# A one-pass gate, a later set-up, and expert outputs added in pairs on VectorE

## The chip, the cores and the metric

The kernel runs on one core of one Trainium2 chip. The metric is device time in microseconds (us) for the whole program: three runs of the kernel before took 2207.76, 2207.96 and 2212.83 us, median 2207.96.

## The reference, cut to what matters

A batch of 16 images (64 channels, 128 x 128) goes through three stages, all in fp32. 1024 image tokens come from deformable attention, 128 text tokens are appended, so each image has 1152 tokens of 64 channels.

```
q_feat = bilinear_sample(image, grid);  q = q_feat @ W_q.T
off    = gelu(layer_norm(q_feat @ W_o1 + b_o1)) @ W_o2 + b_o2      # 8 points for each query
s      = bilinear_sample(image, grid + 4 * off);  k = s @ W_k.T;  v = s @ W_v.T
h      = concat(softmax(q . k) @ v, txt)                           # [16, 1152, 64]
h      = h + Re(C_w @ state) + d_vec * n(h)    # time axis is the batch: 16 steps, state per token
x      = n(h)                                  # n: normalisation over the 64 channels
logits = x @ gate_w + gate_b;  disp = the two largest, their probabilities scaled to sum 1, else 0
out    = h + sum over 16 experts e of disp[e] * ((silu(x @ w1[e]) * (x @ w2[e])) @ w3[e])
```

All 16 experts (hidden size 128) are computed for every token and weighted by `disp`.

## The kernel before, in words

The loop is over the 16 images. Tokens are handled in 9 tiles of 128, three tiles to a group (`GT = 3`, a group is 384 columns), so there are three groups to an image. Every engine runs an order of work that is written out by hand, one letter to a piece of work, in `ORDER` (lines 167 to 254); `KINDS` names the letters. Each engine is strictly in order, and semaphores join them. Stages of image b+1 (map, gather, attention) stand between the expert work of image b. No planner runs at build time.

The kinds of work that matter here, with their letters:

- `A1` (a): TensorE turns the map, four rows at a time, ScalarE stores it (`pixmaj`, line 913); `A2` (b) samples the grid. `B0` to `B6` compute offsets and the gather indices `idx`. On SyncE `L` (p) loads the map, `Q` (C) writes a quarter of the table of pixels to HBM. On GpSimd `G` (o) gathers points from the table (line 601), two indirect DMAs and a short memset (`rest`, line 608) at a time, 64 indirect DMAs to an image; `B1` (e) there computes one power.
- `D1` (k) on VectorE weights the four corners of gathered points (`wsam`, line 1138), `D2` (l) transposes them on TensorE and adds the corners, `D3` (m) makes keys and values, `S1` to `S3` and `D5` are the attention. `gath` has two buffers.
- `P1` to `P6` are the norms and the state update of a group. `P7` (z) is the gate: `xsplit` holds a token's x in 64 partitions rounded to fp32r and in the other 64 the rest; for each of the three tiles TensorE runs two matmuls with 16 columns into the same 16 columns of `bank_p`, one with the rounded gate weights, one with their rest (line 736); VectorE then adds the bias (line 1100) and finds the two largest. `P8` makes `disp`, `P9` transposes it.
- `X` (J), 16 to a group: four matmuls for h1 and h2 of one expert (lines 658, 659; three PSUM banks in turn), ScalarE's silu (842), VectorE's product into `hid` (1038), which has `HB = 4` slots.
- `R` (D), 8 to a group: TensorE spreads `disp` of two experts over 128 partitions, ScalarE stores it in `wide` (882).
- `W` (I), 8 to a group: TensorE makes the outputs of two experts in `bank_o`, one expert in each half of the partitions (667); VectorE multiplies by `wide` into `scaled[n % SB]` (1045), `SB = 5` buffers. The next `W` waits for that product, as `bank_o` is one bank.
- `Z` (K), 2 to a group: TensorE transposes four `scaled` buffers and adds them in `bank_z`, three tiles by four buffers, 12 matmuls (677). `M2` (q) on VectorE adds the two halves and the residual into `ob` (1057, 1058), and SyncE stores it.

At the start SyncE issues constants in four parts between the map's loads (`load_constants`). With them come `w1` and `w2` in raw form, 2 MB in four DMAs into the two `gath` buffers, and `w3` (0.5 MB). VectorE waits for all constants, splits `w1` and `w2` into rounded part and rest (`w12`, lines 960 and 961), and computes the phases of the state. TensorE's `setup()` stands before the first `A2` and waits for `setup_done`, which VectorE gives at line 987; ScalarE's `setup()` stands there as well. GpSimd's first gather waits for `setup_done` too, since the raw weights lie in `gath`.

Of the kernel before, what the change touches and what calls it, by code (L numbers as in the profile page):

```python
# [34 lines left out]
C = 64  # L35
# [10 lines left out]
NE = 16  # L46
# [11 lines left out]
HB = 4  # L58
PAIRS = NE // 2
HALF = PAIRS // 2  # L60
SB = 5
# [19 lines left out]
def grid():  # L81
# [87 lines left out]
        "aaaaaaaaaaaaaaaabbbbbbbbcdehiaaaaaaalalmmlaaalammllmamalaabbbbbbbblcmdmellmhmilaltmumvalaaalxamzJmaJ",  # L169
        "lJaBaDJIDJaDJlDImDJImDJalDJIDJKaJalamJmIlJJtIulvJmJImlxIzJKJaJBalDbJImDJImDJblDJIDJbDbJlDJmDImtJlubb",  # L170
        "bvJKIlbJmcJmdexlzIJlJImBJmDJlDIDJDDJKDIlDJmDJItmulJvhJiIJlJImamaJxaJKIJzaIJaJaJaaIBJDJDIDlDJKDJIDlDJ",
        "mDJItmuJlvJIJlJImJxmJKIlJzaJlIJmaBJmIDaJDlDIDJaDlJDamDJKDItmJuaJlIaJlvIJamJbmbJIbbbJbxbJKIblJzIlJcmJ",
        "BmJIDdDJlDJIDeDlDJmDJKDItmJuJlIJlvhJiImJamJaIJxaJKIJzaIJaaJJaaIBJDJDIDlDJKDJIDlDJIDmtJmuJlvJIJlIJmJx",
        "mJKIlJzaJlIJmaBJmIDaJDlJDIDalDJaDmJDKDItmJuaJlIaJlvIJamJbmbJIbbbJbxbJKIblJzIlJcmJBmJIDdDJlDJIDeDlDJm",
        "DJKDItmJuJlIJlvhJiImJamJaIJxaJaKIJzIaJaJaJaIBJDJDIlDJKDJIDlDJmDJIDmtJluJIvJlJImJKmxJIlJzaJlIJmaBJmID",
        "aJDlDIDJaDlJDamDJKDItmJuaJlIaJlvIJamJbmbJIbbbJbxbJKIblJzIlJcmJBmJIDdDJlDJIDeDlDJmDJKDItmJuJlIJlvhJiI",
        "mJamJaIJxaJKIJzaIJaaJJaaIBJDJDIlDJKDJIDlDJmDJIDmtJluJIvJlJImJKmxJIlJzaJlIJmaBJmIDaJDlDIDJaDlJDamDJKD",
        "ItmJuaJlIaJlvIJamJbmbJIbbJbbxbJKIblJzIlJcmJBmJIDdDJlDJIDeDlDJmDJKDItmJuJlIJlvhJiImJamJaIJxaJKIJzaIJa",
        "aJJaaIBJDJDIlDJKDJIDlDJmDJIDmtJluJIvJlJImJKmxJIlJzaJlIJmaBJmIDaJDlDJIDalDJaDmJDKDItmJuaJlIaJlvIJamJb",
        "mbJIbbbJbxbJKIblJzIlJcmJBmJIDdDJlDJIDeDlDJKDmDJItmJuJlIJlvhJiImJamJaIJxaJKIJzaIJaJaJaaIBJDJDIlDJKDJI",  # L180
        "DlDJIDmDJmtJluJIvJlJImJKmxJIlJzaJlIJmaBJmIDaJDlDJIDalDJaDmJDKDItmJuaJlIaJlvIJamJbmbJIbbJbbxbJKIblJzI",
        "lJcmJBmJIDdDJlDJIDeDlDJKDmDJItmJuJlIJlvhJiImJamJaIJxaJKIJzaIJaaJJaaIBJDJDIlDJKDJIDlDJmDJIDmtJluJIvJl",
# [120 lines left out]
def build(nc, x, txt, wq, wk, wv, w_o1, b_o1, ln_g, ln_b, w_o2, b_o2, nu, theta, bmat, cmat, dvec,  # L303
          gamma, gate_w, gate_b, w1, w2, w3, ident, stack, pick_in, refpx, interp, phase, out):
    with ExitStack() as ctx:
# [101 lines left out]

        const_in = sem("const_in")
        eye_in = sem("eye_in")
        raw_in = sem("raw_in")  # L410
        setup_v = sem("setup_v")
        setup_p = sem("setup_p")
        setup_a = sem("setup_a")
# [875 lines left out]
```

## Time and profile before

| | |
|---|---|
| runs, median (lowest to highest) | 2207.96 us (2207.76 to 2212.83) |
| the profiled execution, its own time | 2205.73 us |
| its span | 2203.9 us |
| TensorE matmul busy | 92% of the span |
| TensorE weight load busy | 70% |
| VectorE busy | 81% |
| ScalarE busy | 54% |
| GpSimd busy | 69% |
| mean granted TensorE clock | 0.977 of full speed |

The profile is one execution. Busy time of an engine is the union of its instructions, and what is left is waiting or the time between instructions. Weight loads overlap matmuls. `L677` is line 677 of the kernel before.

### The profile page before, as it was taken

To read this page: it belongs to the slowest core of one execution; us is meant where nothing else is said; L and a number is where in the kernel's file an instruction comes from. 1 tells how busy PE (TensorE), PEld (TensorE's weight loads), DVE (VectorE), ACT (ScalarE), POOL (GpSimd) and SP (SyncE) were. 2 spreads that over 40 slices of the span, in tenths; PEclk is the share of its full clock that TensorE was granted. 3 is DMA by queue.
4 is the path that set the end of the run, shared out by engine and by line. 5 is a ranking of instruction groups with operands and counts; after the bars stand their busy time and mean duration, and the time that the engine had idled before them with its cause. 6 is when DMAs were issued, how large, how long until landed. Compare 5 with 4: busy or idle time off the path is not lost.

```text
span 2203.9 us, 42639 instructions
## 1 busy us (share of the span) xinstructions
PE 2028.7 (92%) x13857; PEld 1541.3 (70%) x13857; DVE 1775.4 (81%) x4292; ACT 1184.9 (54%) x3048; POOL 1513.4 (69%) x1753
## 2 busy tenths in 40 slices
PE   2468999999999999999999999999999999999998
PEld 1346677777777777777777777777777677776765
DVE  1346788888889888888988888898988889898875
ACT  1225555555565555655555565555556556654553
POOL 0378778778686867868676786868688686868700
PEclk9778999999999999999999999999999999999999
DMA  8786726667654656656464666646476664632200
GB/s 196 218 240 171 214 74 186 178 179 197 168 156 116 188 161 186 195 165 174 121 192 133 188 197 172 184 121 194 119 201 176 179 191 126 184 95 75 71 3 6
DMA packets 363274, 346.61 MB, mean 157 GB/s; under 512 B 49456, under 2 KB 313776, under 8 KB 362928
## 3 DMA queue, kind: packets, MB, share of 16 engines
q1 hardware_dynamic: 313904, 209.60, 34.9%
q0 software_dynamic: 49152, 134.28, 21.0%
q8 instruction: 114, 1.87, 0.4%
q14 instruction: 104, 0.85, 0.1%
HBM read 205.90 MB, written 137.89 MB: 156 GB/s over the span
## 4 chain that ended last, share of the span: by engine, by line
PE 67%; DVE 12%; POOL 10%; issue 8%; ACT 2%; DMA 1%; POOLq 0%; DVEq 0%; ACTq 0%; SPq 0%
PE bank_h L658 11%; PE bank_o L667 10%; PE bank_h L659 9%; PE bank_d L748 9%; PE bank_d L758 9%; POOL gath L601 7%; PE bank_z L677 4%; PE bank_p L694 4%; PE bank_a L770 2%; DVE hid L1038 2%; DVE v_sb L1166 2%; DVE v_sb L1173 2%; PE bank_p L713 2%; PE bank_p L718 1%; POOL rest L608 1%
## 5 line engine op out<-in xcount | busy, mean ns | idle before, releaser
L601 POOL DMA_INDIRECT gath<-table,idx x1024 | 1133.9, 1107 | 258.5 <-issue 239.8
L658 PE MATMUL bank_h<-xsplit,w 128*128 128x384 f32 x1536 | 587.5, 382 | 18.7 <-DVE hid L1038 17.5
L659 PE MATMUL bank_h<-xsplit,w 128*128 128x384 f32 x1536 | 521.1, 339 | 0.0
L842 ACT ACTIVATE silu<-bank_h 128x384 f32<-128x384 f32 x768 | 382.5, 498 | 241.7 <-PE bank_h L659 239.7
L1038 DVE TENSOR_TENSOR hid<-silu,bank_h 128x384 f32<-128x384 f32 x768 | 419.9, 550 | 82.0 <-ACT silu L842 74.0
L658 PEld LDWEIGHTS bank_h<-xsplit,w 128*128 128x128 f32 x1536 | 293.0, 191 | 118.8 <-issue 63.8
L1138 DVE TENSOR_TENSOR wsam<-gath,cw 128x1024 f32<-128x1024 f32 x256 | 313.0, 1223 | 53.0 <-PE bank_d L748 27.0
L667 PE MATMUL bank_o<-hid,w_sb 128*64 128x384 f32 x1536 | 334.7, 514 | 12.2 <-DVE scaled L1045 10.8
L748 PE MATMUL bank_d<-eye,wsam 128*128 128x128 f32 x2048 | 275.7, 279 | 25.3 <-DVE wsam L1138 24.8
L659 PEld LDWEIGHTS bank_h<-xsplit,w 128*128 128x128 f32 x1536 | 293.7, 191 | 3.2
L758 PE MATMUL bank_d<-w_kv,samT 128*128 128x256 f32 x1024 | 278.5, 395 | 5.6 <-ACT v_sb L898 2.7
L748 PEld LDWEIGHTS bank_d<-eye,wsam 128*128 128x128 f32 x2048 | 237.5, 143 | 63.0 <-DVE wsam L1138 41.9
L882 ACT COPY wide<-bank_p 128x384 f32<-128x384 f32 x384 | 185.0, 482 | 161.8 <-PE bank_p L694 161.2
L770 PE MATMUL bank_a<-eye,xin 128*128 128x128 f32 x1024 | 171.4, 294 | 76.9 <-DMA xin<-x_dram 43.4
L621 POOL TENSOR_SCALAR lns<-lns 128x3 f32<-128x3 f32 x96 | 39.1, 408 | 293.4 <-ACT lnsq L848 289.4
L913 ACT COPY pixmaj<-bank_a 128x512 f32<-128x512 f32 x256 | 150.2, 587 | 139.9 <-PE bank_a L770 137.6
L1045 DVE TENSOR_TENSOR scaled<-bank_o,wide 128x384 f32<-128x384 f32 x384 | 212.2, 553 | 12.2 <-PE bank_o L667 8.1
L758 PEld LDWEIGHTS bank_d<-w_kv,samT 128*128 128x128 f32 x1024 | 181.3, 193 | 51.8 <-issue 22.1
L608 POOL MEMSET rest<- 1x400 f32 x512 | 215.9, 422 | 0.2
L770 PEld LDWEIGHTS bank_a<-eye,xin 128*128 128x128 f32 x1024 | 127.2, 149 | 114.7 <-issue 56.3
L1144 DVE TENSOR_TENSOR k_sb<-k_sb,q_sb 128x256 f32<-128x256 f32 x256 | 108.3, 423 | 114.8 <-ACT v_sb L898 114.0
L894 ACT COPY k_sb<-bank_d 128x256 f32<-128x256 f32 x256 | 95.3, 372 | 156.1 <-PE bank_d L758 155.0
(157 smaller groups left out, 2704.4 us busy)
## 6 DMA issues: line engine op xcount, KB each, us to landing
table<-pixmaj SPq DMA_DIRECT2D x80, 1024.0 KB, 9.7
xin<-x_dram SPq DMA_DIRECT2D x256, 256.0 KB
table<-pixmaj SPq DMA_DIRECT2D x32, 960.0 KB
table<-pixmaj SPq DMA_DIRECT2D x16, 1088.0 KB
gath<-table,idx POOLq DMA_INDIRECT x1024
out_dram<-ob SPq DMA_DIRECT2D x48, 96.0 KB, 7.0
gath<-w_dram SPq DMA_DIRECT2D x4, 512.0 KB, 9.5
interp_sb<-interp_dram SPq DMA_DIRECT2D x1, 1024.0 KB, 5.2
```

The source lines that it names most:

```text
L601: pool.indirect_dma_start(out=gath[buf][:, p, :, :].rearrange("p a c -> p (a c)"), out_offset=None, in_=table[par], in_offset=bass.Indirec ...
L608: nc.gpsimd.memset(rest[:], 0.0).then_inc(rested, 1)
L658: mm(bank[:, 0:GC], w12[:, e, which, 0, :], xsplit[gp][:], start=True, stop=False)
L659: mm(bank[:, 0:GC], w12[:, e, which, 1, :], xsplit[gp][:], start=False, stop=True).then_inc(ready, 1)
L667: last = mm(bank_o[C * h:C * (h + 1), 0:GC], w3_sb[:, 2 * q + h, :], hid[:, (2 * n + h) % HB, :], start=True, stop=True)
L748: last = mm(bank_d[:, 128 * (2 * f + pair):128 * (2 * f + pair + 1)], wsam[:, corner, 2 * pair:2 * pair + 2, :].rearrange("p n c -> p (n c)"),
L758: last = mm(bank_d[:, 256 * i:256 * (i + 1)], samT[:, 2 * f + i, :], w_kv[:], start=True, stop=True)
L770: last = mm(bank_a[:, 128 * r:128 * (r + 1)], xin[u % 2][:, HW * (4 * (c % 2) + r):HW * (4 * (c % 2) + r + 1)], eye[:], start=True, stop=T ...
L842: nc.scalar.activation(silu[e % 2][:], bank_h[r][:, 0:GC], ACT.Silu).then_inc(silu_done, 1)
L1038: tt(hid[:, n % HB, :], silu[e % 2][:], bank_h[r][:, 0:GC], ALU.mult).then_inc(hid_done, 1)
L1045: tt(scaled[n % SB][:], bank_o[:, 0:GC], wide[:, q, :], ALU.mult).then_inc(eo_scaled, 1)
L1138: tt(wsam[:].rearrange("p a n c -> p n a c"), gath[j % GB][:, 4 * f:4 * f + 4, :, :], spread(w, 3, C), ALU.mult).then_inc(weighted, 1)
```

## The change

Four edits.

1. **Pairs.** The product of an even `W` goes into one of two `paired` buffers, that of an odd `W` into `odd`; right behind an odd one VectorE adds `odd` into the even one's buffer. `Z` then transposes and adds two buffers instead of four, 6 matmuls instead of 12. `odd` is one buffer and `SB` is 2.
2. **Gate.** For each tile one matmul with 32 columns, the rounded gate weights and their rest side by side, instead of two with 16. VectorE adds the second half in an instruction of its own.
3. **Set-up.** The raw weights no longer go to `gath` but to `wide` and `hid`, and their DMAs, with that of `w3`, are issued after the fourth quarter of the first table. VectorE's phases, splits and rotation, ScalarE's and TensorE's parts of the set-up move into the `D1` and `D2` pieces of the first image. The first gather and the first `A2` no longer wait for the set-up, the first `X` waits for the splits.
4. **`HB = 6`** instead of 4, and new strings in `ORDER` for all five engines, with the same number of each letter. In an inner image the strings differ by a few neighbours changing places; at the start they differ more (GpSimd: 24 letters `o` between the first two `e` instead of 20).

```diff
-HB = 4
+HB = 6
-SB = 5
+SB = 2
-        scaled = [sb(f"scaled{i}", [128, GC]) for i in range(SB)]
+        paired = [sb(f"paired{i}", [128, GC]) for i in range(SB)]
+        odd = sb("odd", [128, GC])
...
# W on VectorE
-                        wait(dve, mix_ready, (n - SB) // HALF + 1)
-                        tt(scaled[n % SB][:], bank_o[:, 0:GC], wide[:, q, :], ALU.mult).then_inc(eo_scaled, 1)
+                        if q % 2:
+                            dve.wait_ge(eo_paired, n // 2)
+                        else:
+                            wait(dve, mix_ready, (n // 2 - SB) // 2 + 1)
+                        mine = odd if q % 2 else paired[n // 2 % SB]
+                        tt(mine[:], bank_o[:, 0:GC], wide[:, q, :], ALU.mult).then_inc(eo_scaled, 1)
+                        if q % 2:
+                            dve.wait_ge(eo_scaled, n + 1)
+                            even = paired[n // 2 % SB]
+                            tt(even[:], even[:], odd[:], ALU.add).then_inc(eo_paired, 1)
# Z on TensorE
-                        pe.wait_ge(eo_scaled, n + HALF)
+                        pe.wait_ge(eo_paired, (n + HALF) // 2)
...
-                            for q in range(HALF):
+                            for q in range(0, HALF, 2):
# P7 on TensorE and VectorE
-                            for part in range(2):
-                                last = mm(bank_p[:, NE * k:NE * (k + 1)], xsplit[gp][:, 128 * k:128 * (k + 1)],
-                                          gate_r[:, part, :], start=part == 0, stop=part == 1)
+                            last = mm(bank_p[:, 2 * NE * k:2 * NE * (k + 1)], xsplit[gp][:, 128 * k:128 * (k + 1)],
+                                      gate_r[:].rearrange("p a e -> p (a e)"), start=True, stop=True)
...
+                        link(top, tt(logit[:], parts[:, :, 1, :], logit[:], ALU.add))
# set-up: SyncE, TensorE, ScalarE, GpSimd, VectorE
-        raw_w = [gath[0][:].rearrange("p a b c -> p (a b c)"), gath[1][:].rearrange("p a b c -> p (a b c)")]
+        raw_w = [(0, 0, NE, flat[:, 0:NE * HID]), (1, 0, NE // 2, flat[:, NE * HID:NE * HID * 3 // 2]),
+                 (1, NE // 2, NE, hid[:].rearrange("p a b -> p (a b)")[:, 0:NE // 2 * HID])]
...
+                        if b == 0 and args[0] == 3:
+                            for dst, src in raw_loads:
+                                sp.dma_start(dst, src).then_inc(raw_in, 16)
...
+                        if n == 0:
+                            pe.wait_ge(split_v, 2 * len(raw_w))
...
+                        if b == 0 and (j, f) == (1, 1):
+                            setup()
...
-                if k == 0 and b == 0:
-                    pool.wait_ge(setup_done, 1)
...
+                            if (j, f) == (1, 0):
+                                setup_phases()
+                            elif (j, f) == (3, 0):
+                                setup_rot()
+                            elif (j, f) in ((1, 1), (2, 0), (2, 1)):
+                                split_weights(2 * j + f - 3)
```

## Rows read from the trace of the kernel before

**Rows 1.** The page, part 1: busy time and share of the span by engine.

```profile
PE 2028.7 (92%) x13857; PEld 1541.3 (70%) x13857; DVE 1775.4 (81%) x4292; ACT 1184.9 (54%) x3048; POOL 1513.4 (69%) x1753
```

**Rows 2.** By window: length, busy PE, PEld, DVE, ACT, POOL, then PEclk, DMA share, GB/s.

```profile
400.00:1800.00 1400.00, 1360.18 (x9531) 1046.39 (x9530) 1208.70 (x2927) 811.82 (x2092) 1043.77 (x1201) 1.00 0.60 168
```

**Rows 3.** Groups of TensorE, 400 to 1800 us: busy us, mean ns, idle before.

```profile
L677 PE MATMUL bank_z<-eye,scaled 128*128 128x128 f32 x792 | 97.4, 273 | 0.2
L736 PE MATMUL bank_p<-gate_r,xsplit 128*128 128x16 f32 x198 | 24.1, 242 | 0.0
```

**Rows 4.** VectorE's waits, 400 to 1800 us, first and last of 11: total, times, longest.

```profile
DVE k_sb L1144 <- ACT v_sb L898: 59.9, 63, 1.4
...
DVE dispr L1126 <- DVE disp L1123: 0.2, 1, 0.2
```

**Rows 5.** Groups of VectorE over the whole span, by shape.

```profile
L1045 DVE TENSOR_TENSOR scaled<-bank_o,wide 128x384 f32<-128x384 f32 x384 | 212.2, 553 | 12.2 <-PE bank_o L667 8.1 <-ACT wide L882 0.8
L1026 DVE TENSOR_TENSOR x2n<-lnx,lns 128x384 f32<-128x384 f32 x48 | 26.6, 555 | 13.9 <-POOL lns L624 13.7
L1100 DVE TENSOR_TENSOR logit<-bank_p,gateb 128x48 f32<-128x48 f32 x48 | 9.7, 202 | 2.2 <-PE bank_p L736 2.1
L1187 DVE TENSOR_TENSOR off_b<-off_a 128x128 f32<-128x128 f32 x16 | 4.7, 293 | 0.5
L961 DVE TENSOR_TENSOR w<-gath,w 128x2048 fp32r<-128x2048 f32 x2 | 4.6, 2293 | 0.1
```

**Rows 6.** Busy time by window over one image, columns as in rows 2.

```profile
1000.00:1021.20 21.20, 21.20 (x138) 17.22 (x138) 18.97 (x52) 11.88 (x35) 16.03 (x19) 1.00 0.33 88
1021.20:1042.40 21.20, 21.20 (x156) 16.57 (x155) 17.03 (x30) 15.42 (x37) 18.20 (x19) 1.00 0.90 249
1042.40:1063.60 21.20, 21.01 (x218) 16.21 (x216) 18.88 (x53) 10.28 (x29) 17.90 (x24) 1.00 0.66 194
1063.60:1084.80 21.20, 21.20 (x130) 16.46 (x130) 18.19 (x49) 11.54 (x32) 7.37 (x8) 1.00 0.08 20
1084.80:1106.00 21.20, 17.75 (x110) 12.95 (x110) 20.51 (x55) 13.50 (x31) 18.09 (x21) 1.00 0.81 227
1106.00:1127.20 21.20, 21.20 (x127) 15.48 (x127) 16.73 (x32) 11.01 (x32) 17.18 (x23) 1.00 0.79 232
```

**Rows 7.** Busy time by window at the start and the end, columns as in rows 2.

```profile
0.00:70.00 70.00, 17.56 (x64) 11.45 (x64) 12.45 (x26) 11.02 (x21) 1.00 (x9) 1.00 0.88 216
80.00:90.00 10.00, 2.49 (x9) 1.42 (x8) 5.32 (x20) 1.09 (x4) 1.65 (x1) 0.57 0.00 1
90.00:130.00 40.00, 22.98 (x100) 16.82 (x100) 10.38 (x17) 10.51 (x22) 33.37 (x40) 0.67 0.99 277
200.00:400.00 200.00, 187.47 (x1231) 141.26 (x1229) 165.96 (x387) 114.00 (x292) 157.64 (x184) 0.99 0.63 179
2094.00:2203.90 109.90, 99.37 (x525) 65.32 (x523) 76.31 (x203) 49.38 (x130) 5.26 (x10) 0.97 0.02 5
```

**Rows 8.** Instructions in order of time at the start: start us, us, idle before.

```profile
27.19 7.40 SPq L554 DMA_DIRECT2D gath<-w_dram  x4
...
71.59 0.42 PE L640 MATMUL bank_p<-eye,b_st 128*64 128x128 f32 x1 [4.10 <-DVE hid L987]
...
90.56 1.24 POOL L601 DMA_INDIRECT gath<-table,idx  x1 [6.56 <-DVE idx L1218]
...
155.68 1.68 POOL L616 TENSOR_TENSOR off_s<-off_s,neghalf 128x8 f32<-128x8 f32 x1 [6.03 <-DVE off_s L1189]
```

**Rows 9.** A gather beside a VectorE instruction with two operands in SBUF.

```profile
161.22 2.23 DVE L1166 TENSOR_TENSOR v_sb<-v_sb,score 128x2048 f32<-128x2048 f32 x1
...
161.68 2.58 POOL L601 DMA_INDIRECT gath<-table,idx  x1 [0.30 <-issue]
```

**Rows 10.** Groups of GpSimd, 400 to 1800 us.

```profile
L601 POOL DMA_INDIRECT gath<-table,idx x705 | 783.5, 1111 | 173.2 <-issue 165.3 <-DVE idx L1218 7.5 <-DVE wsam L1138 0.3
L621 POOL TENSOR_SCALAR lns<-lns 128x3 f32<-128x3 f32 x66 | 27.3, 413 | 174.1 <-ACT lnsq L848 171.1
```

More of the change, by code:

```diff
@@ L540, in out_group @@
                              ob[gp][:]).then_inc(out_done[gp], 16)
-            raw_loads = [(raw_w[n][C * half:C * (half + 1), :].rearrange("c (e h) -> c e h", e=NE),
-                          w.rearrange("e c h -> c e h")) for n, w in enumerate((w1, w2)) for half in range(2)]
+            raw_loads = [(raw[C * half:C * (half + 1), :].rearrange("c (e h) -> c e h", h=HID),
+                          (w1, w2)[which][first:last].rearrange("e c h -> c e h"))
+                         for which, first, last, raw in raw_w for half in range(2)]
+            raw_loads.append((w3_sb[:], w3.rearrange("e h o -> h e o")))
             loads = [(dst, src, const_in) for dst, src in const_loads]
-            loads += [(dst, src, raw_in) for dst, src in raw_loads]
             loads += [(dst, src, const_in) for dst, src in block_loads]
@@ L955, in _ @@
             step(nc.vector.memset(state[:], 0.0))
-            dve.wait_ge(raw_in, 64)
-            for n in range(2):
-                raw = raw_w[n].rearrange("p (e h) -> p e h", e=NE)
-                step(vcopy(w12[:, :, n, 0, :], raw))
-                step(tt(w12[:, :, n, 1, :], raw, w12[:, :, n, 0, :].bitcast(F32), ALU.subtract))
             step(vcopy(sel[:].rearrange("p (e c) -> p e c", c=C), spread(lnsq[:, 0, 0:NE], 2, C)))
@@ new lines, in setup_rot, with split_weights @@
+            def setup_rot():
+                dve.wait_ge(setup_a, 6)
+                step(ts(col[:, 14:16], col[:, 14:16], col[:, 7:8], None, ALU.mult))
+                step(ts(rot[:, 0:C], eye2[:], col[:, 14:15], None, ALU.mult))
+                step(ts(rot[:, C:128], eye2[:], col[:, 15:16], None, ALU.mult))
+                dve.wait_ge(setup_done, 1)
+                assert su.n == SETUP_V
+            def split_weights(n):
+                which, first, last, raw = raw_w[n]
+                raw = raw.rearrange("p (e h) -> p e h", h=HID)
+                high = w12[:, first:last, which, 0, :]
+                if n == 0:
+                    dve.wait_ge(raw_in, 16 * (2 * len(raw_w) + 1))
+                vcopy(high, raw).then_inc(split_v, 1)
+                dve.wait_ge(split_v, 2 * n + 1)
+                tt(w12[:, first:last, which, 1, :], raw, high.bitcast(F32), ALU.subtract).then_inc(split_v, 1)
@@ L1112, in run @@
                         g = args[0]
-                        top.start(b, TOP_N * g + 4)
+                        top.start(b, TOP_N * g + 5)
                         dve.wait_ge(gap_tanh, NGRP * b + g + 1)
```

242 lines of the change are left out of this document (123 added, 119 removed).

## The prediction

> **What bounds the kernel now.** I read the page's busy times first. TensorE's matmuls fill 92% of the span and VectorE 81% [rows 1]. Between 400 and 1800 us TensorE is busy 1360.18 of 1400 us, VectorE 1208.70 [rows 2]. The 792 transposes of line 677 there are 11 images of 72 [rows 3], so an image takes 1400/11 = 127.3 us. Of that TensorE works 1360.18/11 = 123.7 and stands 3.6; VectorE works 109.9 and stands 17.4. The list of waits says how the 17.4 divide: its eleven pairs sum to 148.5 us, 13.5 to an image, the longest for ScalarE's `v_sb` [rows 4]; the other 42.8, or 3.9 to an image, are short pauses between dependent instructions that no engine can take away. So VectorE's floor is 113.8, TensorE's 123.7, and TensorE sets the pace. The windows of one image show that it isn't so everywhere. In five of six TensorE is full; in the fifth it is busy 17.75 of 21.20 and VectorE 20.51, the softmax [rows 6].
>
> The start is another regime. Until 90 us the first map, the constants and the first table go through the DMA engines (share 0.88, 216 GB/s to 70 us), TensorE is busy a quarter of the time, and between 80 and 90 us the DMA engines do nothing at all [rows 7] while offsets are computed; the first gather starts at 90.56 [rows 8]. Then gathers pace the work until TensorE fills; it is busy 187.47 of the 200 us from 200 on [rows 7], so this is at about 210. After 2094 there is only expert work, TensorE busy 99.37 of 109.90 [rows 7].
>
> **Pairs, on TensorE.** 792 matmuls of line 677 are busy 97.4 us [rows 3], 0.123 each. 36 of 72 to an image go: 36 x 0.123 = 4.4 us. **Gate.** 198 matmuls are busy 24.1 us, 0.122 each, whether that is 16 columns or the weight load of 128x128 [rows 3]. 9 of 18 to an image go, 1.1 us; the wider ones cost between nothing and twice their price (then the gain is nil); I take nothing, since 128 columns in line 677 cost the same 0.123. TensorE's work falls to 123.7 - 5.5 = 118.2.
>
> **What VectorE gets.** Twelve additions to an image, 128x384, both operands in SBUF. The same shape from SBUF took 555 ns, with one operand in PSUM 553 [rows 5]; bounds from further off are 293 ns for 128 columns and 2293 for 2048. I take 0.555, less 0.01 of overlap, plus the pause behind the odd product it waits for, 0.5 us over 16 [rows 5] or 0.03: 0.58 x 12 = 6.9 us. The gate's second addition is 0.20, with its pause 0.24, three to an image [rows 5]: 0.7. I sum them with slightly longer pauses to 7.9 (7.6 by the rows alone, 0.3 for the new wait of an even product on `Z`). The floor of VectorE becomes 113.8 + 7.9 = 121.7. So the two engines change places: 118.2 against 121.7.
>
> **The sum over the windows.** A mean floor is only reached if work can move freely. I add to each window of rows 6 a sixth of VectorE's additions and pauses, (7.9 + 3.9)/6 = 1.97, take 5.5/6 = 0.92 from TensorE, and keep the larger:
>
> - 20.9, 20.3, 20.9, 20.3, 22.5, 20.3. VectorE sets the first, third and fifth, TensorE the rest.
>
> They sum to 125.2, against 127.3: 2.1 us less to an image. The softmax window gets longer by 1.3, the others shorter. The order strings could spread VectorE's load (down to 121.7), and waits that neither floor holds could add (3.6 as now); I let these cancel. From 210 to 2094 us there are 1884/127.3 = 14.8 images: 14.8 x 2.1 = 31 us.
>
> **New waits.** With two pair buffers the third pair of a group waits for the whole first `Z`, which waits for the addition. Behind the waiting product on VectorE stand `hid` products, for which TensorE's `W` and, through the three banks, its `X` wait. Before, the fifth product needed no `Z`, the sixth did. The price is 0 where `Z` has run in time, and up to one `Z` (0.74) six times, 4.4 us, where not; I take the 0.3 above, as line 677 hardly idled (0.2 us in 792) [rows 3]. `HB = 6` I cost at nothing: `hid` waits for silu and not for a slot in any long wait; it may give back some of TensorE's wait on `W`. What ScalarE does is unchanged and its load is 54% [rows 1].
>
> **The start.** 2.5 MB of raw weights leave the stretch to 70 us: at its 216 GB/s [rows 7] that is 11.7 us. Their four big issues also hold SyncE's queue for 7.40 us [rows 8] in front of the fifth load of the map; that lies within the 11.7. The first `A2` no longer waits behind the set-up: TensorE stood 4.10 us for line 987 [rows 8], most of it saved, 3.7. The seven raw DMAs now go out behind the last quarter of the table, into the 10 idle us of the DMA engines; behind them on SyncE stand loads of the second map, which TensorE does not need before the gathers run. VectorE's splits go between the first `D1`s: two of 2048 columns at most 2.29 each, four of 1024 at most half that, below 9.2 us, and the phases and rotation 17 short ones of some 0.2, or 3.7. VectorE is busy 10.38 of 40 us there [rows 7], so they are hidden; if a third came into the gathers' path, it would be 4 us. GpSimd stood 6.03 us at 155.68 for an operand of its power [rows 8]; four more `o` (eight gathers) stand in front of that now, so part of this wait goes, between 0 and 6.0, I take 3. In 90 to 130 us the DMA engines are at 0.99 [rows 7], so not all of the earlier start survives; I take 1.4 off. Start: 11.7 + 3.7 + 3 - 1.4 = 17 us, bounds 4 and 22.
>
> **The end.** Over 109.9 us VectorE has room (76.31) [rows 7]; TensorE's 5.5 to an image is 5.5 x 109.9/127.3 = 4.8 us. At the very last `Z` an addition of 0.58 comes in and 0.74 goes.
>
> **The time.** 17 + 31 + 5 = 53 us. The profiled execution took 2205.7 us with its span of 2203.9; 2205.7 - 53 = 2152.7. The median of the runs lies 2.3 above it, so 2155.
>
> **Rivals.**
>
> - *All of TensorE's saving arrives.* The strings were rewritten for all engines, and VectorE's longest waits are for TensorE's results, which now come sooner [rows 4]. Then VectorE's floor of 121.7 plus a few tenths is the pace: 5.2 x 14.8 = 77, with start and end 99 us: 2109. Against it speaks window five.
> - *Only the start and the end gain.* The stages that VectorE bounds lose what the others gain: 22 us, 2186.
> - *VectorE's waits stay: slower.* Place: the middle of each image; in order behind each `W`, VectorE's added 7.9 pushes `hid`, TensorE's `X` waits, and VectorE still stands for `v_sb` and silu. If all 13.5 of waits stay, an image takes 121.7 + 13.5 = 135.2. It decides from 127.3 + 22/14.8 = 128.8, so from 7.1 of the 13.5 still left. With 9 left: 130.7, 3.4 x 14.8 = 50 - 22, so 2236. For it speaks that these waits are many and short (63 times, at most 1.4 us) [rows 4]; against it that an engine that runs late waits less. Weight loads are busy 1046.39 of 1400 us, 75%, VectorE 86% [rows 2]. The Trainium skill ("Perfetto Trace Analysis", Identifying the Most-Contended Engine) holds matmul busy time a bad measure, since matmuls are pipelined, and wants weight-load share instead; by it VectorE is the bound already, the 5.5 are worth nothing and the 7.9 are paid. By the windows [rows 6], where TensorE has no gap in four of six, I don't follow it.
> - *Gathers slow down.* A gather that began beside a VectorE instruction of 2.23 us with both operands in SBUF took 2.58 us instead of a mean of 1.111 [rows 9, 10]. The additions are 12 more such instructions, 12 x 0.55 = 6.6 us to an image on GpSimd. It is busy 1043.77/11 = 94.9 and spends 15.0 between gathers: 109.9 + 6.6 = 116.5, still under 125.2. Only if its 15.6 us of waits for the norms [rows 10] stay too is it 132.1, 4.8 x 14.8 = 71 - 22 slower: 2257. The Trainium skill ("SBUF — State Buffer", SBUF: two separate sides) says that a VectorE instruction with two SBUF inputs holds a port pair that GpSimd shares, and shuts it out for its whole length; on this rows 9 agree.
>
> **Chances.** Forecast 0.60; all of it 0.13; start and end only 0.12; VectorE's waits 0.11; gathers 0.04. The forecast's own range is 2130 to 2180. For 8 in 10 I take 2110 to 2195, which leaves out the two slower cases and a little of the first rival. A difference of 0.3%, 6.6 us, is about what a measurement can tell: faster 0.84, within it 0.04, slower 0.12.
>
> **What would show it.** Between 400 and 1800 us line 677 has 36 matmuls to an image and TensorE's share falls to 94 to 95%, VectorE's rises from 86% to about 94%; VectorE's waits for `v_sb` and silu shrink to about half. The additions last 0.55 us. TensorE now has waits on `hid` and on the pair addition. The first gather starts near 75 us. I am wrong if VectorE's share stays below 90% while the time hardly falls (its waits stayed), if the mean gather goes above 1.25 us, or if the first gather is not before 80 us.

## The result, and the profile after

The changed kernel took 2187.72 us (median of 4 runs, 2184.80 to 2189.38) against 2207.86 (4 runs, 2206.97 to 2212.83) for the kernel before on the same chip: ratio 0.9899, 95% interval 0.9880 to 0.9918. It is 20 us faster, where 53 us were forecast. The time lies inside the range given for 8 in 10 (2110 to 2195) and outside the forecast's own (2130 to 2180). Runs more than 1.5% above the fastest of the same kernel are left out of every ratio. The profiled span is 2187.6 us, 16.3 less than before.

To see where the 16.3 us fell I take VectorE's instruction that writes an image's gather indices (`idx`), once per image. First the row of the kernel before, then of the changed one, from the fourth image to the last; "a to b" are the first and last start in us.

```profile
L1218 DVE SCALAR_TENSOR_TENSOR idx<-xyf x13: 224/225/227, 447.4 to 1973.8; 128x64 int32<-128x64 f32 x13
```

```profile
L1262 DVE SCALAR_TENSOR_TENSOR idx<-xyf x13: 224/225/227, 428.5 to 1953.5; 128x64 int32<-128x64 f32 x13
```

Up to the fourth image the changed kernel is 18.9 us ahead. The twelve images between take 1525.0 instead of 1526.4 us: 127.08 each instead of 127.20. From the last `idx` to the end of the span it takes 234.1 instead of 230.1. So: start -18.9, middle -1.4, end +4.0. The forecast had -17, -31 and -5 (its middle began at 210 us). The middle is what failed.

The page's busy times and the window of the middle (400 to 1800 us), as in [rows 1] and [rows 2]:

```profile
PE 1978.7 (90%) x13137; PEld 1472.8 (67%) x13137; DVE 1866.7 (85%) x4534; ACT 1183.3 (54%) x3048; POOL 1518.2 (69%) x1753
```

```profile
400.00:1800.00 1400.00, 1331.77 (x9038) 1002.80 (x9037) 1270.86 (x3094) 809.62 (x2093) 1045.44 (x1201) 0.98 0.60 168
```

TensorE's busy time fell by 28.4 us over these 11 images, VectorE's rose by 62.2, and TensorE now stands idle for 68.2 us where it stood for 39.8. The granted clock is 0.98 where it was 1.00.

Part 4 of the page follows the work that ended last back through whatever released it. The shares of that chain, in the kernel before and then in the changed one:

```profile
PE 67%; DVE 12%; POOL 10%; issue 8%; ACT 2%; DMA 1%; POOLq 0%; DVEq 0%; ACTq 0%; SPq 0%
```

```profile
PE 41%; DVE 26%; POOL 20%; issue 11%; ACT 1%; DMA 1%; DVEq 0%; POOLq 0%; ACTq 0%
```

TensorE carried two thirds of the chain and now carries two fifths; VectorE and GpSimd have about doubled. No engine sets the pace of the changed kernel alone.

The groups that the change touches (busy us, mean ns, idle before; 400 to 1800 us), as in [rows 3, 5, 10]:

```profile
L688 PE MATMUL bank_z<-eye,paired 128*128 128x128 f32 x396 | 56.3, 279 | 0.1
L746 PE MATMUL bank_p<-gate_r,xsplit 128*128 128x32 f32 x99 | 13.2, 234 | 0.0
L1081 DVE TENSOR_TENSOR paired<-paired,odd 128x384 f32<-128x384 f32 x132 | 73.9, 560 | 4.5
L1077 DVE TENSOR_TENSOR paired<-bank_o,wide 128x384 f32<-128x384 f32 x132 | 72.9, 552 | 1.9 <-PE bank_z L688 0.5 <-PE bank_o L678 0.3
L608 POOL DMA_INDIRECT gath<-table,idx x706 | 796.8, 1129 | 174.0 <-issue 165.4 <-DVE idx L1262 8.4 <-DVE wsam L1182 0.2
```

The reader sees 36 transposes to an image instead of 72, 9 gate matmuls instead of 18, 12 additions of 0.56 us, and gathers that hardly got longer (1129 against 1111 ns). The waits of TensorE and then of VectorE in the same stretch (total us, times, longest):

```profile
PE bank_o L678 <- DVE odd L1077: 21.2, 12, 1.9
PE bank_h L667 <- DVE hid L1066: 13.9, 23, 0.8
PE bank_a L782 <- ACT pixmaj L932: 8.4, 11, 0.8
```

```profile
DVE k_sb L1188 <- ACT v_sb L917: 29.9, 43, 1.4
DVE hid L1066 <- ACT silu L857: 25.8, 47, 1.0
DVE x2n L1054 <- POOL lns L631: 17.0, 15, 3.3
```

`v_sb` fell from 59.9 [rows 4] to 29.9, as forecast; TensorE's longest wait is now for a scaled product: 21.2 us, where the kernel before had 8.1 us in 11 waits. The windows of one image, as in [rows 6], show where it lies:

```profile
972.00:993.20 21.20, 21.20 (x123) 15.56 (x122) 17.08 (x32) 10.62 (x32) 17.19 (x21) 1.00 0.34 102
993.20:1014.40 21.20, 20.78 (x127) 16.07 (x126) 18.75 (x55) 14.57 (x40) 17.76 (x23) 1.00 0.68 185
1014.40:1035.60 21.20, 21.13 (x237) 15.27 (x236) 19.82 (x36) 12.19 (x28) 18.18 (x21) 1.00 0.96 278
1035.60:1056.80 21.20, 21.20 (x136) 17.03 (x135) 20.37 (x62) 13.26 (x38) 14.51 (x15) 1.00 0.20 57
1056.80:1078.00 21.20, 20.43 (x119) 14.55 (x117) 20.38 (x52) 13.27 (x32) 9.67 (x13) 1.00 0.26 68
1078.00:1099.20 21.20, 16.85 (x92) 13.05 (x93) 19.87 (x53) 10.23 (x27) 17.20 (x20) 0.92 1.04 294
```

In the last window, the softmax stretch, TensorE is busy 16.85 us (17.75 before), and there the clock is 0.92. TensorE's instructions in order of time (start, us, idle before) show the pause and what follows:

```profile
1082.25 0.33 PE L667 MATMUL bank_h<-xsplit,w 128*128 128x384 f32 x1
1082.42 0.34 PE L668 MATMUL bank_h<-xsplit,w 128*128 128x384 f32 x1
1082.60 0.60 PE L782 MATMUL bank_a<-eye,xin 128*128 128x128 f32 x4
1085.13 0.87 PE L678 MATMUL bank_o<-hid,w_sb 128*64 128x384 f32 x4 [1.94 <-DVE odd L1077]
...
1088.37 0.53 PE L668 MATMUL bank_h<-xsplit,w 128*128 128x384 f32 x1
1088.68 0.53 PE L667 MATMUL bank_h<-xsplit,w 128*128 128x384 f32 x1
...
1090.83 0.34 PE L705 MATMUL bank_p<-dispT,sel 128*128 128x384 f32 x1
```

A matmul of 384 columns takes 0.34 us before the pause and 0.53 behind it, and the next one starts 0.31 us later instead of 0.17: the granted clock is 1.2 instead of 2.4 GHz there. Adding up the stretches in which half speed was granted, between 400 and 1800 us: 13.7 us in the kernel before (4 stretches), 58.0 us in the changed one (13 in 11 images). My estimate is that half of such a stretch is lost: 6.8 against 29.0 us of full-speed work, 0.6 against 2.6 to an image.

VectorE's instructions in the same pause say what it stands for. The first row is the sum over the eight samples (three additions), the third the product that TensorE's `bank_o` waits for:

```profile
1081.66 2.40 DVE L1217 TENSOR_TENSOR v_sb<-v_sb 128x1024 f32<-128x1024 f32 x3
1084.10 0.43 DVE L1221 TENSOR_TENSOR h_sb<-v_sb,sden 128x256 f32<-128x256 f32 x1
1084.44 0.55 DVE L1077 TENSOR_TENSOR odd<-bank_o,wide 128x384 f32<-128x384 f32 x1
```

VectorE did these three in this order in the kernel before too. There TensorE had two pieces of the map (`a`) in front of that `W`, and waited little:

```profile
1098.90 0.60 PE L770 MATMUL bank_a<-eye,xin 128*128 128x128 f32 x4
1100.27 0.63 PE L770 MATMUL bank_a<-eye,xin 128*128 128x128 f32 x4 [0.77 <-ACT pixmaj L913]
1101.44 0.87 PE L667 MATMUL bank_o<-hid,w_sb 128*64 128x384 f32 x4 [0.54 <-DVE scaled L1045]
```

TensorE's old string has `aaI` at this place in 11 of 13 images. The new one has `JaI` in all 13, with one `a` moved elsewhere. So the pause of 1.9 us in front of this `W` comes with the new strings; the experiments bear this out.

### The profile page after: what moved, and what is told of

Read it like the earlier page. It is cut to its first block, busy times and chain, and to the rows that moved or that the text cites. A ratio compares the mean times of both kernels' runs of the same rounds, so it can differ in the third digit from the quotient of the medians.

```text
span 2187.6 us, 41444 instructions
## 1 busy us (share of the span) xinstructions
PE 1978.7 (90%) x13137; PEld 1472.8 (67%) x13137; DVE 1866.7 (85%) x4534; ACT 1183.3 (54%) x3048; POOL 1518.2 (69%) x1753
## 4 chain that ended last, share of the span: by engine, by line
PE 41%; DVE 26%; POOL 20%; issue 11%; ACT 1%; DMA 1%; DVEq 0%; POOLq 0%; ACTq 0%
POOL gath L608 15%; PE bank_h L667 7%; PE bank_o L678 6%; PE bank_h L668 6%; PE bank_d L760 6%; PE bank_d L770 5%; DVE hid L1066 4%; POOL rest L615 3%; DVE wsam L1182 3%; PE bank_p L705 3%; DVE v_sb L1217 2%; DVE v_sb L1210 2%; PE bank_z L688 1%; PE bank_a L782 1%; POOL lns L631 1%
## 5 line engine op out<-in xcount | busy, mean ns | idle before, releaser
L608 POOL DMA_INDIRECT gath<-table,idx x1024 | 1153.1, 1126 | 256.3 <-issue 239.5
L667 PE MATMUL bank_h<-xsplit,w 128*128 128x384 f32 x1536 | 594.0, 387 | 30.1 <-DVE hid L1066 26.9
L668 PE MATMUL bank_h<-xsplit,w 128*128 128x384 f32 x1536 | 526.6, 343 | 0.0
L667 PEld LDWEIGHTS bank_h<-xsplit,w 128*128 128x128 f32 x1536 | 297.7, 194 | 139.1 <-issue 69.9
L678 PE MATMUL bank_o<-hid,w_sb 128*64 128x384 f32 x1536 | 339.9, 520 | 34.8 <-DVE odd L1077 26.6
L668 PEld LDWEIGHTS bank_h<-xsplit,w 128*128 128x128 f32 x1536 | 298.5, 194 | 2.5
L628 POOL TENSOR_SCALAR lns<-lns 128x3 f32<-128x3 f32 x96 | 34.3, 357 | 274.5 <-ACT lnsq L863 270.1
L705 PE MATMUL bank_p<-dispT,sel 128*128 128x384 f32 x384 | 163.9, 427 | 2.5 <-ACT wide L897 2.3
L678 PEld LDWEIGHTS bank_o<-hid,w_sb 128*64 128x64 f32 x1536 | 78.7, 137 | 117.1 <-issue 98.7
```

The lines of the kernel that those rows point to most:

```text
L608: pool.indirect_dma_start(out=gath[buf][:, p, :, :].rearrange("p a c -> p (a c)"), out_offset=None, in_=table[par], in_offset=bass.Indirec ...
L667: mm(bank[:, 0:GC], w12[:, e, which, 0, :], xsplit[gp][:], start=True, stop=False)
L668: mm(bank[:, 0:GC], w12[:, e, which, 1, :], xsplit[gp][:], start=False, stop=True).then_inc(ready, 1)
L678: last = mm(bank_o[C * h:C * (h + 1), 0:GC], w3_sb[:, 2 * q + h, :], hid[:, (2 * n + h) % HB, :], start=True, stop=True)
L705: mm(bank_p[:, 0:GC], sel[:, 128 * q:128 * (q + 1)], dispT[:], start=True, stop=True).then_inc(wide_ready, 1)
```

## The experiments

Kernels were measured in five series, each on one chip with the kernel before beside them (the recorded expectations say "call"). In the last three series the kernel before took about 2210 us, and the traces of the edited kernels look like the two above. In the first two, with eight kernels on two chips, it took about 2380 us, and their traces have waits that nothing in the kernel ends (releaser `remote`). So every time is read against the kernel before of its own series. Two of these waits in the changed kernel, 400 to 1800 us:

```profile
ACT silu L857 <- remote: 36.8, 17, 7.2
ACT k_sb L913 <- remote: 13.0, 9, 2.2
```

### Two series with the kernel before at 2380 us

The edits, each on the changed kernel:

```
# no_add, no_add_again: an addition becomes a memset of 8 columns (the odd products are missing from the output)
-    tt(even[:], even[:], odd[:], ALU.add).then_inc(eo_paired, 1)
+    nc.vector.memset(odd[:, 0:8], 0.0).then_inc(eo_paired, 1)
# old_order, old_order_again: the ORDER strings of the kernel before
# u_pairs: pairs undone (scaled[n % 5], 12 transposes to a Z, HB = 4); order, gate, set-up new
# setup_gate: u_pairs with the old ORDER strings
# setup_only: setup_gate with the two-pass gate
```

> The changed kernel with the twelve additions to an image left out (the odd product is computed and not added, so the output lacks half of the expert outputs; 8 columns are cleared instead, to keep the signal). Theory A, VectorE is the bound between 400 and 1800 us now: it loses 12 x 0.56 = 6.7 us to an image less 12 short clears of some 0.07, so an image falls from 127.1 to 121 to 124 us and the time to 2115 to 2150. Theory B, the pace is set by GpSimd's order (gathers behind the waits for the norms) or another chain that the additions are not on: 2175 or more.

> The later set-up and the one-pass gate alone, with the order strings of before, four-buffer Z, SB = 5, HB = 4. Theory A (the pairs cost VectorE what they give TensorE): the start's 16 us and up to 1.1 us of TensorE to each of 15 images, so 2175 to 2190, no slower than the whole change. Theory B (pairs give something, the gain is lost in a fixed chain): 2192 to 2197, slower than the whole change.

> The later set-up alone, with the order strings of before. Both theories: the first index list comes some 15 us earlier, and 2208 - 12 to 16 = 2192 to 2196. If the strings of before give part of the start away again at GpSimd's wait (6 us), 2198 to 2202.

> The changed kernel with the order strings of before. Theory A: Z stands too early in TensorE's old order for the pair addition, TensorE waits more: 2195 to 2230. Theory B: the strings matter little in the middle, 2185 to 2195.

Measured in one series (before 2384.13): `no_add` 2285.13, ratio 0.9578 (0.9546 to 0.9610); `setup_gate` 2367.48, 0.9919 (0.9880 to 0.9959); `setup_only` 2369.82, 0.9933 (0.9902 to 0.9965); `old_order` 2330.72, 0.9792 (0.9750 to 0.9833). The changed kernel was not beside them, so its part in the 0.958 can't be told from these runs.

> The changed kernel itself, beside the others on one chip: the reference for this call. If TensorE runs here as in the first trace, 0.990 of the kernel before. If TensorE is held up more than there, as in the four runs of the call before (TensorE busy 89% of a span of 2366 us, with pauses of 1 to 2 us before single instructions), what lightens TensorE is worth more: 0.975 to 0.985.

> The changed kernel with the order strings of before, now beside the changed kernel. Theory A (Z stands too early for the addition): 1 to 2% slower than the changed kernel. Theory B (the strings matter little, the pairs do): within 0.5% of it.

> The changed kernel with the pairs undone: four scaled buffers to a Z, SB = 5, HB = 4, the new strings, the one-pass gate and the later set-up kept. Theory A (VectorE bounds the middle now, and the pairs take what they give): the same time as the changed kernel within 0.5%, TensorE's share back at 96 to 97%. Theory B (the pairs are a gain, the strings lose it): 1 to 2% slower than the changed kernel.

> The changed kernel with the twelve additions to an image left out, so that the output lacks half of the expert outputs, now beside the changed kernel. Theory A: an image falls from 127.1 to 121 to 124 us, 2 to 4% under the changed kernel. Theory B (a chain the additions are not on): within 0.7% of it.

Measured (before 2379.49): `after_again` 2259.95 and 2261.66, 0.9496 (0.9415 to 0.9577), its other two runs 2296.59 and 2303.89; `old_order_again` 2326.31, 0.9780 (0.9717 to 0.9842); `u_pairs` 2363.44, 0.9928 (0.9869 to 0.9986); `no_add_again` 2287.88, 0.9604 (0.9541 to 0.9667). There the change is worth 5% by its two lower runs. Undoing the pairs gives 103 of these 119 us back, and leaving out the additions gains nothing: it lies 27 us above the two lower runs, within the spread of all four. That is another regime, and nothing on the runs at 2210 us follows from it; all runs below have the kernel before at 2209 to 2213.

### Dummy work against the clock, and VectorE relieved

```
# fill: dummy transposes before six pieces of every order stretch "zIJaaJaJaI" (in 13 images), 3 5 3 5 12 4, 32 in all
+    if at.get(step, 0):          # at: the table of places; turned: the last D3 piece done (neither shown)
+        wait(pe, kv_stored, turned)
+    for _ in range(at.get(step, 0)):
+        mm(bank_d[:, 384:512], eye[:], eye[:], start=True, stop=True, is_transpose=True)
# no_vsum: the sum over samples on 2 of 32 columns
-    link(soft, tt(vw[:, :, 0:n, :], vw[:, :, 0:n, :], vw[:, :, n:2 * n, :], ALU.add))
+    link(soft, tt(vw[:, :, 0:n, 0:2], vw[:, :, 0:n, 0:2], vw[:, :, n:2 * n, 0:2], ALU.add))
# hb5_sb3
-HB = 6, SB = 2
+HB = 5, SB = 3
```

> The changed kernel itself, to compare the others of this call with. On the chip of its first profile it took 0.990 of the kernel before, on another chip 0.950, where TensorE is held up more. Here between 0.945 and 0.992.

> The changed kernel, with 32 dummy transposes of 128x128 per image (about 0.12 us each, 3.9 us in all) issued at six places of the softmax stretch where TensorE otherwise stands for VectorE and ScalarE, 6 us to an image. Theory C: what eats the forecast gain of the middle is the granted clock, which falls to half once per image just behind these pauses and costs 29.0 us of full-speed work between 400 and 1800 us instead of 6.8 before. Then the dummy work keeps the clock up and the time falls by 1 to 2 us per image, 15 to 25 us in all, or 0.7 to 1.1% against the changed kernel in this call, with less than half as much time at half clock. Theory V: VectorE's own chain sets the pace of the whole middle and the half clock hides beneath it. Then nothing comes back, and where a dummy outlasts the pause the kernel loses up to 1 us per image (0 to 15 us slower), even if the clock stays up.

> Leaves out nearly all of the sum over eight samples behind the softmax: three additions of 128x1024, 512, 256 columns (2.40 us together) shrink to 2 of 32 columns of each block, twice per image. VectorE's longest stretch without product or hid loses some 2 us each time. If VectorE in the softmax stretch is the pace and its pause costs the clock as well (theory C), the time falls by more than the 4 us per image that are left out: 4 to 5 per image, 60 to 75 us, 2.7 to 3.3% against the changed kernel. If VectorE's total work sets the pace (theory V), 4 per image, 55 to 60 us. If TensorE's count of instructions alone sets it and the pause does not matter, under 10 us.

> Three pair buffers instead of two and five silu-product buffers instead of six. If the new wait of an even product on Z (two buffers) is what holds the middle, it goes and the time falls by up to 0.5 us per image, 7 us (0.3%). By theories C and V alike nothing changes beyond 0.3%: TensorE waited 4.5 us in 12 times for a product into a pair buffer, 0.4 per image, of which only a part is for the buffer.

Measured (before 2212.69): changed kernel 2185.22, 0.9884 (0.9863 to 0.9906); `fill` 2174.01, 0.9834 (0.9813 to 0.9856); `no_vsum` 2164.12, 0.9777 (0.9752 to 0.9802); `hb5_sb3` 2185.17, 0.9893 (0.9862 to 0.9924).

`fill` adds work and is 11.2 us faster than the changed kernel. The `idx` rows of the changed kernel, `fill` and `no_vsum`, measured side by side; a twelfth of each stretch is an image, 126.76, 125.81 and 125.54 us:

```profile
L1262 DVE SCALAR_TENSOR_TENSOR idx<-xyf x13: 224/225/228, 425.8 to 1946.9; 128x64 int32<-128x64 f32 x13
```

```profile
L1280 DVE SCALAR_TENSOR_TENSOR idx<-xyf x13: 224/225/228, 425.5 to 1935.2; 128x64 int32<-128x64 f32 x13
```

```profile
L1262 DVE SCALAR_TENSOR_TENSOR idx<-xyf x13: 224/226/227, 425.6 to 1932.1; 128x64 int32<-128x64 f32 x13
```

The window of the middle of `fill` and TensorE's waits:

```profile
400.00:1800.00 1400.00, 1366.30 (x9480) 1035.11 (x9478) 1278.62 (x3128) 818.38 (x2118) 1053.29 (x1211) 1.00 0.60 169
```

```profile
PE bank_o L696 <- DVE odd L1095: 6.9, 11, 0.6
PE bank_h L685 <- DVE hid L1084: 5.4, 30, 0.3
```

The clock is back at 1.00 (3.4 us at half speed instead of 64.9 in the changed kernel beside it), and an image takes 125.81 instead of 126.76 us. The gain is below the 15 to 25 us of theory C. The dummies cost 50.4 us of TensorE in the middle (0.143 each, not 0.12); that some of it lay outside the pauses would explain the difference, but was not measured. Theory V, that the half clock hides beneath VectorE, is refuted, unless the dummies help by shifting TensorE's later work in time; no run adds such a shift and leaves the clock down.

`no_vsum` shrinks 4.7 us of additions per image to short ones of 1.1, so VectorE loses 3.6 us. 4 to 5 were expected back; 1.2 came (125.54), though the clock stayed up (6.8 us at half speed). `fill` got 1.0 with the clock up; if the clock is worth as much here, hardly anything is left for VectorE's 3.6 us. The pause in front of `W` is gone (one wait of 0.5 us for `odd`), so the sum over samples is what it stood for. Most of the 3.6 us turned into another wait of VectorE, which in the changed kernel beside it was 15.2:

```profile
DVE x2n L1054 <- POOL lns L631: 49.9, 22, 3.9
```

All three theories had the size wrong: even in the softmax stretch neither engine alone sets the pace. `hb5_sb3` is no faster (126.61 us to an image): a third pair buffer, with five `hid` slots instead of six, changes nothing.

### Additions, pairs and order, with the kernel before at 2209 us

The edits are those above; `fill_no_add` is `fill` with the additions left out as in `no_add`.

> The dummy transposes of the run before, and the twelve additions of an image left out (a memset of 8 columns on VectorE stands for each, so the output lacks the odd products). If VectorE's added work is what still holds an image at 125.8 us once the clock stays up (theory V), its 6.7 us to an image bring a good part of themselves: 2 us or more per image, 30 us and more, 0.969 of the kernel before or less. If what is left are waits that run through several engines (theory L: the norms from GpSimd, the softmax stretch, the order), it gives under 1 us per image, 0.976 to 0.983.

> The changed kernel with the pairs undone: eight scaled products in five buffers, 72 transposes of line 677 to an image, no additions, four silu-product buffers; the new order, gate and set-up stay. Theory C: TensorE's 4.4 us to an image come back, VectorE's 6.7 go, and TensorE no longer pauses so long in the softmax stretch, so the clock stays up: an image takes 127 to 128.5 us and the time is within 1% of the changed kernel's, 0.985 to 0.998 of the kernel before, with under half of the half-clock time. Theory T (TensorE's work alone counts, as on the chips where it is held up): 4.4 x 14.8 = 65 us slower than the changed kernel, 1.018 of the kernel before.

> The changed kernel without its twelve additions to an image (the output lacks the odd products). Theory C and L: the softmax stretch is VectorE's own softmax work, so TensorE's pause there stays and the clock still falls: under 1.5 us per image, 0.978 to 0.99 of the kernel before, and more than 25 us at half clock between 400 and 1800 us. Theory V: the additions are the pace, 3 to 5 us per image, 0.965 or less, and the clock stays up.

> The changed kernel with the order strings of the kernel before. Theory O: the rewritten strings carry part of the gain, as on the other chips (2%), through shorter waits: 1.00 to 1.01 of the kernel before, with TensorE waiting more than 10 us per image. Theory C: the strings matter less here; the start keeps most of its 16 us, an image takes 127 to 128 us, 0.99 to 1.0.

Measured (before 2209.39): `fill_no_add` 2151.83, 0.9733 (0.9717 to 0.9749); `u_pairs_once_more` 2196.05, 0.9939 (0.9922 to 0.9955); `no_add_once_more` 2164.93, 0.9792 (0.9776 to 0.9808); `old_order_once_more` 2216.47, 1.0028 (1.0012 to 1.0043). The `idx` rows of the last image stretch, in this order:

```profile
L1279 DVE SCALAR_TENSOR_TENSOR idx<-xyf x13: 224/225/227, 429.5 to 1922.9; 128x64 int32<-128x64 f32 x13
```

```profile
L1252 DVE SCALAR_TENSOR_TENSOR idx<-xyf x13: 224/224/226, 427.7 to 1958.7; 128x64 int32<-128x64 f32 x13
```

```profile
L1261 DVE SCALAR_TENSOR_TENSOR idx<-xyf x13: 224/225/226, 431.2 to 1934.1; 128x64 int32<-128x64 f32 x13
```

```profile
L1262 DVE SCALAR_TENSOR_TENSOR idx<-xyf x13: 224/226/228, 444.6 to 1978.4; 128x64 int32<-128x64 f32 x13
```

An image takes 124.45, 127.58, 125.24 and 127.82 us. Without the additions an image is 1.5 us shorter than the changed kernel's 126.76 (of the series before). They cost VectorE 6.7 (73.9/11 in the group above), and the memsets in their place 0.8, so 5.9 us are gone. So theory V, 3 to 5 us per image, is out; theory C's "under 1.5" is just met or just missed. With the clock kept up, `fill_no_add` is 1.4 us per image shorter than `fill`: between theory L (under 1) and theory V (2 or more), so both had it wrong. Without additions, TensorE's pause and the clock stay as they were: `bank_o` <- `odd` is still 21.2 us, and 58.0 us at half speed. The clock and the additions are nearly independent: the additions are worth 20.3 us without dummies (2185.2 to 2164.9) and 22.2 with them (2174.0 to 2151.8; the times of each pair are of two series, with before at 2212.7 and 2209.4). Undoing the pairs costs 11 us, as theory C had it. But its half-clock time, 44.4 us, is not under half of the changed kernel's, so the clock falls there too, without any addition. TensorE's wait in front of `W` in `setup_gate_once_more` (old strings, eight products), `u_pairs_once_more` (new strings, eight products) and `old_order_once_more` (old strings, pairs) shows with what the pause comes:

```profile
PE bank_o L676 <- DVE scaled L1071: 7.4, 9, 1.9
```

```profile
PE bank_o L676 <- DVE scaled L1071: 19.2, 11, 1.9
```

```profile
PE bank_o L678 <- DVE odd L1077: 7.7, 9, 1.9
```

It is 7 to 8 us with the old strings and 19 to 21 with the new ones, with pairs or without, with additions or without: the pause belongs to the order of work. Half speed was granted for 30.7, 44.4 and 41.0 us in these three, so this pause is a large part of the clock's loss but not all of it.

The old strings lose all of the gain: with them TensorE's waits are spread differently, the longest being

```profile
PE bank_p L695 <- DVE dispr L1164: 19.8, 20, 1.2
PE bank_h L667 <- DVE hid L1066: 17.7, 23, 1.2
```

and the fourth image is only 2.8 us ahead of the kernel before, though the first `idx` is at 76.7 instead of 90.0. Theory O was right on the time, though TensorE stands idle 7.0 us per image where it had said more than 10; theory C on the order was wrong.

### The end, and the set-up without the rest

```
# fill_tail: fill, and 73 dummies more at eight places of the order behind 1930 us
+    at.update({2622: 3, 2624: 16, 2625: 3, 2626: 11, 2627: 4, 2774: 26, 2817: 5, 2819: 5})
```

> The dummy transposes as before, and 73 more at eight places behind 1930 us: the last image's softmax stretch and three later pauses (4.04, 2.33 and 1.69 us are the longest). Theory C: at the end the clock costs 17 us of full-speed work instead of 9.3, and this is why the end did not gain its 5 us. Where the dummies keep it up, the end after the last idx falls from 235 us by 3 to 8, the time is 0.980 to 0.982 of the kernel before. If the end is held by VectorE's hid products and the pair additions in a row, the clock stays up and the time stays that of the run with dummies in the middle only, 0.983, or a little over.

> The order strings and the eight scaled products of the kernel before, with the new set-up and the one-pass gate only. On a chip where TensorE is held up it gave 0.992. With the old strings on top of all changes the third image was only 3 us early, though its first gather was 13 us early: so here, too, the set-up without new strings should bring under 6 us of its 13. Theory C: the gate's 1.1 us per image of TensorE mostly arrive, since VectorE has room (17.4 us per image idle): 10 to 16 us. Together 0.990 to 0.995. If the pairs under the old strings cost nothing of their own, it equals the run with the old strings, 1.003.

Measured (before 2209.79): `fill_tail` 2174.64, 0.9848 (0.9821 to 0.9875); `setup_gate_once_more` 2207.20, 0.9989 (0.9977 to 1.0001). The end of `fill` and then of `fill_tail`:

```profile
1935.00:2170.00 235.00, 211.33 (x1073) 141.74 (x1071) 194.84 (x483) 112.07 (x292) 98.60 (x117) 0.93 0.14 40
```

```profile
1935.00:2170.00 235.00, 218.90 (x1174) 150.91 (x1172) 198.49 (x494) 114.88 (x302) 98.74 (x118) 0.97 0.14 39
```

The half-speed time behind 1935 us fell from 37.3 to 17.1 us, which is some 10 us of full-speed work, but from the last `idx` to the end there are 233.6 instead of 235.5 us, and the time is the same. The 73 dummies are themselves 11.0 us of TensorE there, so this does not show that the clock costs the end nothing; it shows that dummies do not pay there. Leaving out the additions shortens the end to 229.8 us (`no_add_once_more`; 234.0 in the changed kernel of the series before).

`setup_gate_once_more` was expected at 0.990 to 0.995 and is no faster than before. Its `idx` row:

```profile
L1252 DVE SCALAR_TENSOR_TENSOR idx<-xyf x13: 224/225/227, 440.5 to 1971.6; 128x64 int32<-128x64 f32 x13
```

Its fourth image is 6.9 us ahead, and an image takes 127.59 us instead of 127.20, so the gate's 1.1 us of TensorE brought nothing. Part of that is the clock again: 30.7 us at half speed instead of 13.7, up to 0.8 us per image. The four corners, in us (kernel before 2209 to 2213):

| | time | fourth `idx` at | an image | last `idx` to the end |
|---|---|---|---|---|
| old strings, eight products, no additions | 2207.20 | 440.5 | 127.59 | 230.8 |
| old strings, pairs | 2216.47 | 444.6 | 127.82 | 235.8 |
| new strings, eight products, no additions | 2196.05 | 427.7 | 127.58 | 233.9 |
| new strings, pairs | 2185.22 | 425.8 | 126.76 | 234.0 |

All four have the new set-up and gate; `HB` is 4 with eight products and 6 with pairs, and no run separates that. Pairs alone cost 9 us, the strings alone bring 11, both together 22. The strings bring 13 us at the start, nothing in the middle while there are eight products, and cost 3 at the end. The pairs bring 0.8 us per image, 10 us in all, and only under the new strings. Each row is one trace; two traces of the changed kernel differ by 2.7 us at the fourth `idx` and by 0.3 us per image.

## Why the prediction was wrong, point by point

- **TensorE's work: nearly right.** Less what was lost to the clock, an image fell from 123.0 to 118.4 us of TensorE, 4.6 where 5.5 were forecast. The transposes saved 3.7 (0.142 each instead of 0.123), the gate 1.0, where 4.4 and 1.1 were expected.
- **VectorE's additions: right in price** (0.56 us, 6.7 to an image, gate 0.6). VectorE's waits fell from 13.5 to 7.7 us an image, those for `v_sb` and silu together to 58%, near "about half". TensorE's share is 95%, VectorE's 91%, below the 94 but above the 90 I had named.
- **The sum over the windows: this step failed.** It took 2.1 us off an image; 0.1 came (0.4 in the repeat). It has three faults. (1) It carried the clock's loss of before along unchanged. On full-clock terms the forecast was 117.6 us of work, 0.6 lost to the clock and 7.0 idle, 125.2; measured were 118.4, 2.6 and 6.2. So the idle time was nearly right, and 2.0 us more went to the clock and 0.8 to dearer work. The clock falls behind the pause that the new strings opened in front of one `W` of the softmax stretch (0.54 to 1.94 us), and `fill` got 1.0 us per image back by work that is good for nothing else. I had let what the order strings give and what they cost cancel. (2) It paid out TensorE's savings one for one in the stages where TensorE looked full. The gate's 1.1 us alone brought nothing (127.59). With TensorE's 4.7 saved, no addition, and dummies that keep the clock up, an image gains 2.75 (127.20 to 124.45). The chain that ended last went over from TensorE to VectorE and GpSimd; which of their waits holds an image was not shown. (3) It let VectorE's additions vanish wherever VectorE had room. Without them an image is 1.5 us shorter, about a quarter of the 5.9 us that VectorE loses with them, though 127.1 us hold only 119.5 of VectorE's busy time and short pauses. (The six windows sum to 125.1 unrounded, and the text has TensorE full in five of six at one place and in four at another; neither matters.)
- **New waits: right.** Line 688 idled 0.1 us in 396, the products' wait on `Z` is 0.5 us in 11 images, and a third buffer with `HB` at 5 brought nothing. `HB = 6` against 4 was not run by itself.
- **The start: right in size, partly for another reason.** The first `idx` comes 15.1 us earlier (11.7 + 3.7 forecast), the first gather at 75.43 us, and at the fourth image it is 18.9 (17 forecast, bounds 4 and 22). But the set-up alone with old strings keeps 6.9 of it, and with pairs 2.8; the new strings bring the rest. I had put nearly all of it on the moved work.
- **The end: wrong.** 5 were to be gained, 4.0 were lost. The new strings cost 3 of it (230.8 to 233.9 with eight products). The pairs then bring nothing (234.0), since the additions take 4.2 (229.8 without them), about what the halved transposes give. I took VectorE's room of 34 us there as cover for the additions. That they lie on the path from product to `Z` is my reading; the runs show the 4.2 us.
- **The rivals.** "Only the start and the end gain", 2186, came nearest in time (0.12). That is luck in part: it is the start and not the end, and the middle does gain 0.8 us per image from the pairs beside the same strings. The Trainium skill ("Perfetto Trace Analysis", Identifying the Most-Contended Engine) holds matmul busy time a bad measure, and I set that aside; it deserved more. As the prediction read it, TensorE's saved 5.5 us are worth nothing, and the gate's were. It is not the whole, since it lets VectorE's additions be paid in full, and a quarter was. The gathers stayed at 1129 ns, under my mark of 1.25 us; the bad case of one gather in [rows 9] did not become a rule.

The best version is the changed kernel with dummy transposes in the softmax stretch: 2174.01 us, 0.9834 (0.9813 to 0.9856) of the kernel before. That 11.2 us separate it from the changed kernel rests on one series, and `fill_tail`, which holds the same dummies, gave 2174.64 in another. The obvious other cure, to move one `a` back in front of that `W` in TensorE's new string, was not run. What holds an image at 124.5 us with the clock up and the additions out was not found; the waits for GpSimd's norms (49.9 us in `no_vsum`) are where I would look, which no run here tested.

## What to carry to other kernels

When two engines are both nearly full (here 97 and 86% of the middle), work saved on one can be worth a fraction of itself, and work added to the other can cost a fraction of itself: here 2.75 of 4.7 us and 1.5 of 5.9 us. Before a step that lengthens a TensorE pause, look at the granted clock behind the pauses that are already there. A pause can lengthen because one piece of work changed its place. Where it can't be removed, filling it may pay for itself. And measure a data-flow change together with its order of work: pairs were worth +9 us with one order and -11 with the other.

## What the runs showed of the hardware

- The same two kernels differ by 1% in one series and by 5% in another. Where the kernel before took 2380 us, the traces show waits that nothing in the program ends (237 us between 400 and 1800 us in `setup_only`, 110 in the changed kernel's run of 2296.59, none in the first pair of traces). The chip numbered 14 was in one series of each kind, so it may not be the chip itself. The cause is open.
- Half speed cost 29.0 us of TensorE's work between 400 and 1800 us by the estimate above, but its removal brought 11 us of time; whether the rest lies under VectorE's load or went to the dummies themselves wasn't separated. At the end 10 us given back by the clock, less 11.0 us of dummies, brought 2 at most.
- TensorE's clock fell about once per image behind a stretch of five pauses of 0.5 to 1.9 us. The kernel before has a like stretch, with 0.54 us where this one has 1.94, and its clock mostly stayed up. With 32 dummies in them, or with VectorE's sum over samples left out, the changed kernel's stayed up too.
- Twelve more VectorE instructions to an image with both operands in SBUF lengthened the mean gather by 18 ns, 1.6% (1111 to 1129 ns); without them it is 1112 again (`no_add_once_more`).
